# Splitting the key weights behind the first three query units, in the first group of an attention's projections

## The chip, the cores and the metric

The kernel runs on one core of a Trainium2 chip. The engines of that core are TensorE (PE in the profile, with its weight loads as PEld), VectorE (DVE), ScalarE (ACT), GpSimd (POOL) and SyncE (SP), which issues the DMAs. The metric is the device time of one execution in microseconds; less is better.

## The reference, cut to what matters

1024 tokens of width 512 pass through two "macaron" layers: half a feed-forward, an attention, half a feed-forward, each on a layer-normed input and added to the residual `x`. What the change touches is the start of the first layer's attention:

```python
q = hidden_states @ Wq + bq          # hidden 1024 x 512, Wq 512 x 4096
k = hidden_states @ Wk + bk
v = hidden_states @ Wv + bv
q = rms_norm(q, gq)                  # over all 4096 columns
k = rms_norm(k, gk)
...                                  # 32 heads of 128, softmax, values
return out @ Wo + bo
```

All of it is float32. The kernel multiplies at float32 accuracy by splitting both operands into a high part (rounded to a shorter format, `fp32r`) and a low part (the rest), and adding three matmuls: high by high, high by low, low by high.

## The kernel before

The program is a row of blocks with a barrier of all engines between them. The block in question is `qkv_block`. The 4096 columns of each projection are cut in 8 groups of 512 (4 heads). A group runs Q, then K, then V, each as 8 units; a unit is one 128x512 result in one PSUM bank (4 banks in turn), made by 12 matmuls of 512 columns (4 blocks of the width by 3 terms). Group 0 and group 7 are written out, groups 1 to 6 are a loop.

Each engine runs its own list in the order of the code, and waits on semaphores:

- TensorE, unit u: waits until the low part of this projection's weights is there (`w_lo_done`), and until three units less have been taken out of PSUM (`res_done` of at least u - 3 within group 0's Q), then 12 matmuls. In Q of group 0 the weights and the units 0 and 2 were already made at the end of the block before, so TensorE begins with unit 1, goes on with unit 3, and waits for nothing but `res_done` after that.
- VectorE, unit u: `qkv_res` (L826), the unit out of PSUM with the bias added, into one of 4 buffers; in Q then `qkv_q_lo` (L801) of unit u - 1, which needs ScalarE's `qkv_q_hi`.
- ScalarE, unit u: `qkv_q_hi` (L752), the high part of the query times the gain, then `qkv_sq` (L755), the square. The squares have two buffers, so the square of unit u waits until GpSimd has added the square of unit u - 2 (`acc_done`).
- GpSimd: clears its sums, waits for the output bias `bo` by DMA, adds it to the residual `x` in 8 instructions of 128x512 (L855), and only then starts on the group's squares, `qkv_acc` (L865), one per unit of Q and K.
- SyncE: the bias and gain columns, then the key weights `Wk`, `bo`, the value weights `Wv` and a bias; later the stores of the results to DRAM.

In front of each projection's units, ScalarE and VectorE split the weights of the *next* projection: ScalarE `qkv_w_hi` (L734, 128x2048), VectorE `qkv_w_lo` (L767, 128x2048). In group 0 the split in front of the query units is that of the key weights, which are at that time still on their way from DRAM.

Of the kernel before, what the change touches and what calls it, by code (L numbers as in the profile page):

```python
# [54 lines left out]
def wait(eng, sem, value):  # L55

    if isinstance(value, int) and value <= 0:
        return
    eng.wait_ge(sem, value)
# [560 lines left out]
def qkv_block(core, ins, scratch, first):  # L620
# [3 lines left out]
    with ExitStack() as ctx:  # L624
# [6 lines left out]
        Q, K, V = range(3)  # L631
# [26 lines left out]
        k_in, q_in, bo_in, bv_in = sem("k_in"), sem("q_in"), sem("bo_in"), sem("bv_in")  # L658
        kn_done, k0_hi_done = sem("kn_done"), sem("k0_hi_done")

        AT_SUMS, AT_SPREAD = 1, 3
        block = core.open_block(ctx)
        weights = [ins["Wq"], ins["Wk"], ins["Wv"]]
        bias, gain = [core.cols["bq"], core.cols["bk"]], core.cols["gq"]
# [1 line left out]
        def groups(eng, body):  # L666

            body(0)
            with eng.Fori(1, NGROUPS - 1) as g:
                body(g)  # L670
            body(NGROUPS - 1)

        def is_last(g):
            return isinstance(g, int) and g == NGROUPS - 1
# [54 lines left out]
        @block.scalar  # L729
        def _(act):  # L730
            def split(n, t, g):
                act.wait_ge(w_in[t], (g if t == Q else g + 1) * 16)
                wait(act, proj_done, (n - 2) * UNITS - 1)
                nc.scalar.activation(w_hi[t][:], w[t][:], ACT.Copy).then_inc(w_hi_done, 1)  # L734

            def body(g):
                for t in (Q, K, V):
                    n = g * 3 + t
                    if t < V:
                        split(n + 1, t + 1, g)  # L740
                    elif not is_last(g):
                        split(n + 1, Q, g + 1)
                    for u in range(UNITS):
                        if t == V:
                            continue
                        m = g * 16 + t * UNITS + u
                        act.wait_ge(res_done, n * UNITS + u + 1)
                        if t == Q:
                            if u == 0:
                                act.wait_ge(gain_done, g + 2)  # L750
                            wait(act, q_stored[u % 4], (g * 2 + u // 4) * 32)
                            nc.scalar.activation(q_hi[u % 4][:], res[u % 4][:], ACT.Copy,  # L752
                                                 scale=gain_now[:, u // 2:u // 2 + 1]).then_inc(q_hi_done, 1)
                        wait(act, acc_done, m + 2 - 1)
                        nc.scalar.activation(sq[:, u % 2, :], res[u % 4][:], ACT.Square).then_inc(sq_done, 1)  # L755

            groups(act, body)
            act.wait_ge(ms_done, 1)
            nc.scalar.activation(sd, ms, ACT.Sqrt).then_inc(sd_done, 1)
            act.wait_ge(kn_done, 1)  # L760
            nc.scalar.activation(core.first.hi[:], core.kn[:], ACT.Copy).then_inc(k0_hi_done, 1)

        @block.vector
        def _(v):
            def split(n, t):
                v.wait_ge(w_hi_done, n)
                nc.vector.tensor_tensor(w_lo[t][:], w[t][:], w_hi[t][:], ALU.subtract).then_inc(w_lo_done, 1)  # L767

            def factors():

                v.wait_ge(sums_done, 1)
                nc.vector.tensor_scalar(ms, core.bank(6)[:, 0:2 * NT].rearrange("p (a t) -> p a t", a=2),
                                        1.0 / INNER, RMS_EPS, ALU.mult, ALU.add).then_inc(ms_done, 1)
                v.wait_ge(sd_done, 1)
                nc.vector.reciprocal(r0, sd).then_inc(rs_done, 1)
                v.wait_ge(rs_done, 1)
                nc.vector.tensor_tensor(corr, ms, r0, ALU.mult).then_inc(rs_done, 1)
                v.wait_ge(rs_done, 2)
                nc.vector.tensor_tensor(corr, corr, r0, ALU.mult).then_inc(rs_done, 1)
                v.wait_ge(rs_done, 3)  # L780
                nc.vector.tensor_scalar(corr, corr, -0.5, 1.5, ALU.mult, ALU.add).then_inc(rs_done, 1)
                v.wait_ge(rs_done, 4)
                nc.vector.tensor_tensor(rs, r0, corr, ALU.mult).then_inc(rs_done, 1)
                v.wait_ge(rs_done, 5)

                nc.vector.tensor_scalar(core.rq, rs[:, 0, :], float(HD) ** -0.5, None,
                                        ALU.mult).then_inc(rms_done, 1)
                nc.vector.tensor_tensor(diag[:], core.ident[:].unsqueeze(1).broadcast_to([P, NT, P]),
                                        rs[:, 1, :].unsqueeze(2).broadcast_to([P, NT, P]), ALU.mult)\
                    .then_inc(diag_done, 1)  # L790

            v.wait_ge(core.cols_in, 16 * len(core.cols))
            nc.vector.tensor_tensor(gain, gain, core.cols["gk"], ALU.mult).then_inc(gain_done, 1)
            v.wait_ge(gain_done, 1)

            def next_gain(g):
                nc.vector.tensor_copy(gain_now, gain[:, bass.ds(g * GROUP, GROUP)]).then_inc(gain_done, 1)

            def q_low(g, u):
                v.wait_ge(q_hi_done, g * UNITS + u + 1)  # L800
                nc.vector.scalar_tensor_tensor(out=q_lo[u % 4][:], in0=res[u % 4][:],  # L801
                                               scalar=gain[:, bass.ds(g * GROUP + u // 2, 1)], in1=q_hi[u % 4][:],
                                               op0=ALU.mult, op1=ALU.subtract).then_inc(q_lo_done, 1)

            next_gain(0)

            def body(g):
                for t in (Q, K, V):
                    n = g * 3 + t
                    if t < V or not is_last(g):  # L810
                        split(n + 1, (t + 1) % 3)
                    for u in range(UNITS):
                        wait(v, proj_done, n * UNITS + u)
                        if 4 <= t * UNITS + u < UNITS + 4:
                            v.wait_ge(q_lo_done, g * UNITS + t * UNITS + u - 3)
                        else:
                            wait(v, stored[u % 4], (g * 4 + max(t * 2 - 2 + u // 4, 0)) * 16)
                        wait(v, sq_done, g * 16 + max(min(t * UNITS + u - 3, 16), 0))
                        if t == V:
                            if u == 0:  # L820
                                v.wait_ge(bv_in, (g + 1) * 16)
                                if not is_last(g):
                                    next_gain(g + 1)
                            nc.vector.tensor_tensor(res[u % 4][:], core.bank(u % 4), bv[:], ALU.add).then_inc(res_done, 1)  # L824
                        else:
                            nc.vector.tensor_scalar(res[u % 4][:], core.bank(u % 4),  # L826
                                                    bias[t][:, bass.ds(g * GROUP + u // 2, 1)], None, ALU.add)\
                                .then_inc(res_done, 1)
                            if t == Q and u >= 1:
                                q_low(g, u - 1)  # L830
                            elif t == K and u == 0:
                                q_low(g, UNITS - 1)
                        if is_last(g) and t == V and u == AT_SUMS + 1:
                            factors()
                        if is_last(g) and t == V and u == AT_SPREAD + 1:
                            v.wait_ge(spread_done, 1)
                            nc.vector.tensor_copy(core.rk[:], core.ps[2][:]).then_inc(rms_done, 1)

                            v.wait_ge(k_in, 16)
                            v.wait_ge(rms_done, 2)  # L840
                            nc.vector.tensor_tensor(core.kn[:], core.k_raw[:], core.rk[:], ALU.mult)\
                                .then_inc(kn_done, 1)

            groups(v, body)

        @block.gpsimd
# [983 lines left out]
```

## Time and profile before

| | us |
|---|---|
| median of 3 runs | 2322.78 |
| lowest, highest | 2320.69, 2324.09 |
| the profiled execution | 2324.25 |
| its span in the profile | 2322.5 |
| PE busy | 2256.0 (97%) |
| DVE, ACT, POOL busy | 1609.4, 1135.6, 828.8 |
| granted TensorE clock, mean | 0.989 |

The block of the projections takes the span from about 101 to 630 us, the part that the change touches from 101 to 140 us. All times below are microseconds from the start of the span. "Busy" of a matmul overlaps its neighbour's, so the rate of TensorE is read from the distance of the starts. The granted clock is 1.00 at 2.4 GHz and 0.50 at 1.2 GHz.

### The profile page before, as it was taken

To read this page: it belongs to the slowest core of one execution; us is meant where nothing else is said; L and a number is where in the kernel's file an instruction comes from. 1 tells how busy PE (TensorE), PEld (TensorE's weight loads), DVE (VectorE), ACT (ScalarE), POOL (GpSimd) and SP (SyncE) were. 2 spreads that over 40 slices of the span, in tenths; PEclk is the share of its full clock that TensorE was granted. 3 is DMA by queue.
4 is the path that set the end of the run, shared out by engine and by line. 5 is a ranking of instruction groups with operands and counts; after the bars stand their busy time and mean duration, and the time that the engine had idled before them with its cause. 6 is when DMAs were issued, how large, how long until landed. Compare 5 with 4: busy or idle time off the path is not lost. (4 is left out here: it accounts for less than half of the span.)

```text
span 2322.5 us, 34366 instructions
## 1 busy us (share of the span) xinstructions
PE 2256.0 (97%) x11044; PEld 1874.1 (81%) x11044; DVE 1609.4 (69%) x2654; ACT 1135.6 (49%) x1845; POOL 828.8 (36%) x736
## 2 busy tenths in 40 slices
PE   7899999999989999999999999999998999899998
PEld 5688888888778888888888888888886788687887
DVE  5544444444378888888888888888886665785765
ACT  3233332322266666666666666666663344352442
POOL 4553332233222222212212222222214466672565
PEclk9999999999999999999999999999999999999999
DMA  3155555455332211211221221221201111141210
GB/s 114 47 181 191 190 177 183 168 187 184 132 107 71 81 55 67 81 66 56 81 72 50 81 72 50 81 78 44 81 24 41 51 68 44 33 129 37 73 59 37
DMA packets 106182, 210.47 MB, mean 91 GB/s; under 512 B 9728, under 2 KB 42496, under 8 KB 102784
## 3 DMA queue, kind: packets, MB, share of 16 engines
q1 hardware_dynamic: 106112, 209.57, 26.9%
q8 instruction: 39, 0.64, 0.1%
q14 instruction: 31, 0.25, 0.0%
HBM read 140.33 MB, written 69.21 MB: 90 GB/s over the span
## 5 line engine op out<-in xcount | busy, mean ns | idle before, releaser
L1106 ACT ACTIVATE at_pT_hi<-ps 128x512 fp32r<-128x512 f32 x512 | 278.3, 595 | 352.3 <-PE ps L1210 352.2
L1148 DVE TENSOR_REDUCE at_small<-ps 128x1 f32<-128x1024 f32 x256 | 312.5, 1221 | 84.0 <-PE ps L402 83.0
L1158 DVE TENSOR_TENSOR at_pT_lo<-ps,at_pT_hi 128x512 fp32r<-128x512 f32 x512 | 327.1, 680 | 3.8 <-ACT at_pT_hi L1106 3.8
L1113 ACT ACTIVATE at_probs<-ps,at_small,cols 128x1024 f32<-128x1024 f32 x256 | 309.2, 1208 | 28.2 <-DVE at_small L1150 21.6
L865 POOL TENSOR_TENSOR qkv_acc<-qkv_acc,qkv_sq 128x512 f32<-128x512 f32 x128 | 166.2, 1299 | 320.1 <-ACT qkv_sq L755 316.5
L1210 PEld LDWEIGHTS ps<-ident,at_probs 128*128 128x128 f32 x2048 | 239.2, 140 | 37.9 <-issue 4.4
L1210 PE MATMUL ps<-ident,at_probs 128*128 128x128 f32 x2048 | 266.4, 273 | 3.2 <-DVE at_pT_lo L1158 3.2
L1172 DVE SCALAR_TENSOR_TENSOR x<-ps,at_small,x 128x512 f32<-128x512 f32 x256 | 192.0, 750 | 10.2 <-PE ps L402 3.1
L1043 POOL TENSOR_TENSOR at_o_lo<-at_o_raw,at_o_hi 128x512 fp32r<-128x512 f32 x32 | 41.2, 1288 | 439.8 <-ACT at_o_hi L1127 439.8
L402 PE MATMUL ps<-ln_xT_hi,ln_xT_lo 128*128 128x512 f32 x768 | 196.0, 390 | 0.0
L826 DVE TENSOR_SCALAR qkv_res<-ps,cols 128x512 f32<-128x512 f32 x128 | 94.9, 748 | 141.7 <-PE ps L402 122.7
L1235 PE MATMUL ps<-at_pT_hi,ln_xT_lo 128*128 128x512 f32 x512 | 180.6, 393 | 0.7 <-DVE at_y_lo L1144 0.7
L402 PEld LDWEIGHTS ps<-ln_xT_hi,ln_xT_lo 128*128 128x128 f32 x768 | 144.2, 188 | 30.7
L402 PE MATMUL ps<-ln_xT_hi,q_hi 128*128 128x512 f32 x480 | 148.0, 390 | 0.0
L752 ACT ACTIVATE qkv_q_hi<-qkv_res,cols 128x512 fp32r<-128x512 f32 x64 | 46.3, 723 | 194.6 <-DVE qkv_res L826 194.6
L755 ACT ACTIVATE qkv_sq<-qkv_res 128x512 f32<-128x512 f32 x128 | 80.0, 625 | 121.3 <-DVE qkv_res L826 104.8
L402 PE MATMUL ps<-at_o_hi,at_y_hi 128*128 128x512 f32 x256 | 122.0, 477 | 3.9 <-DVE x L1172 3.5
L402 PE MATMUL ps<-ln_xT_hi,first_hi 128*128 128x512 f32 x280 | 113.3, 405 | 7.1 <-DVE ln_xT_lo L282 4.0
L1043 POOL TENSOR_TENSOR ln_xT_hi<-kn,ln_xT_hi 128x1024 fp32r<-128x1024 f32 x31 | 74.2, 2393 | 116.0 <-ACT ln_xT_hi L1083 116.0
L1235 PEld LDWEIGHTS ps<-at_pT_hi,ln_xT_lo 128*128 128x128 f32 x512 | 96.0, 188 | 22.1 <-issue 0.9
L824 DVE TENSOR_TENSOR qkv_res<-ps,qkv_bv 128x512 f32<-128x512 f32 x64 | 43.5, 688 | 98.9 <-PE ps L402 98.8
L402 PE MATMUL ps<-ln_xT_hi,first_lo 128*128 128x512 f32 x280 | 111.1, 397 | 0.0
(273 smaller groups left out, 5636.4 us busy)
## 6 DMA issues: line engine op xcount, KB each, us to landing
scratch_q_hi<-qkv_q_hi SPq DMA_DIRECT2D x64, 256.0 KB, 2.1
scratch_q_lo<-qkv_q_lo SPq DMA_DIRECT2D x64, 256.0 KB, 2.3
scratch_k<-qkv_res SPq DMA_DIRECT2D x64, 256.0 KB, 2.8
scratch_v<-qkv_res SPq DMA_DIRECT2D x64, 256.0 KB, 2.3
k_raw<-scratch_k SPq DMA_DIRECT2D x32, 512.0 KB, 3.8
at_v_raw<-scratch_v SPq DMA_DIRECT2D x32, 512.0 KB, 3.3
wq_raw<-in_Wq SPq DMA_DIRECT2D x8, 1024.0 KB, 6.5
qkv_w<-in_Wk SPq DMA_DIRECT2D x8, 1024.0 KB, 5.0
```

The costliest lines, as they stand in the source:

```text
L402: last = nc.tensor.matmul(out, s, m, start=(start and n == 0), stop=(stop and n == len(terms) - 1))
L755: nc.scalar.activation(sq[:, u % 2, :], res[u % 4][:], ACT.Square).then_inc(sq_done, 1)
L826: nc.vector.tensor_scalar(res[u % 4][:], core.bank(u % 4), bias[t][:, bass.ds(g * GROUP + u // 2, 1)], None, ALU.add)\
L865: nc.gpsimd.tensor_tensor(part, part, sq[:, u % 2, :], ALU.add).then_inc(acc_done, 1)
L1043: nc.gpsimd.tensor_tensor(dst, a, b, ALU.subtract).then_inc(done, 1)
L1106: nc.scalar.activation(pT2[jp][0][:, 4 * b:4 * b + 4, w * P:(w + 1) * P], T_BANKS[:, b * HALF:(b + 1) * HALF].rearrange("p (k n) -> p k n" ...
L1113: nc.scalar.activation(probs[l % 4][:], scores(l)[:], ACT.Exp, bias=nbias[:, l % 4:l % 4 + 1], scale=rq[:, l % NT:l % NT + 1], accum_out=s ...
L1148: nc.vector.reduce_max(maxes[:, l % 4:l % 4 + 1], scores(l)[:], AX.X).then_inc(s_max, 1)
L1158: nc.vector.tensor_tensor(pT2[jp][1][out], T_BANKS[:, b * HALF:(b + 1) * HALF].rearrange("p (k n) -> p k n", k=4), pT2[jp][0][out], ALU.su ...
L1172: nc.vector.scalar_tensor_tensor(out=x[:, tile, :], in0=core.bank(WO_BANK), scalar=rsums[:, c:c + 1], in1=x[:, tile, :], op0=ALU.mult, op1 ...
L1210: last = nc.tensor.transpose(T_BANKS[:, k * P:(k + 1) * P], probs[(l - T_LAG) % 4][:, k * P:(k + 1) * P], core.ident[:])
L1235: last = nc.tensor.matmul(core.bank(PV_BANK), a[:, k, :], b[:, k, :], start=(c == 0 and n == 0), stop=(c == 3 and n == len(terms) - 1))
```

## The change

In Q of group 0 alone (`late`), ScalarE and VectorE no longer split the key weights ahead of unit 0, but between unit 2 and unit 3 (`LATE` is 3). The instructions are the same, 1845 on ScalarE and 2654 on VectorE; nothing of another group moves, and the code of TensorE, GpSimd and SyncE is as it was.

```diff
-        AT_SUMS, AT_SPREAD = 1, 3
+        AT_SUMS, AT_SPREAD, LATE = 1, 3, 3
...
 # ScalarE
                 for t in (Q, K, V):
                     n = g * 3 + t
-                    if t < V:
+                    late = isinstance(g, int) and g == 0 and t == Q
+                    if t < V and not late:
                         split(n + 1, t + 1, g)
-                    elif not is_last(g):
+                    elif t == V and not is_last(g):
                         split(n + 1, Q, g + 1)
                     for u in range(UNITS):
+                        if late and u == LATE:
+                            split(n + 1, t + 1, g)
...
 # VectorE
-                    if t < V or not is_last(g):
+                    late = isinstance(g, int) and g == 0 and t == Q
+                    if not late and (t < V or not is_last(g)):
                         split(n + 1, (t + 1) % 3)
                     for u in range(UNITS):
+                        if late and u == LATE:
+                            split(n + 1, t + 1)
```

ScalarE's list at the start of the block, with the semaphores that each instruction waits on (`qkv_w1` are the key weights, the number in `qkv_res2` is the unit's buffer). Before:

```order
L734 ACTIVATE qkv_w1_hi<-qkv_w1 128x2048 [waits qkv_w_in1]
L752 ACTIVATE qkv_q_hi0<-qkv_res0,cols 128x512 [waits qkv_gain_done,qkv_res_done]
L755 ACTIVATE qkv_sq<-qkv_res0 128x512 [waits qkv_acc_done]
L752 ACTIVATE qkv_q_hi1<-qkv_res1,cols 128x512 [waits qkv_res_done]
L755 ACTIVATE qkv_sq<-qkv_res1 128x512 [waits qkv_acc_done]
L752 ACTIVATE qkv_q_hi2<-qkv_res2,cols 128x512 [waits qkv_res_done]
L755 ACTIVATE qkv_sq<-qkv_res2 128x512 [waits qkv_acc_done]
L752 ACTIVATE qkv_q_hi3<-qkv_res3,cols 128x512 [waits qkv_res_done]
```

The same place after:

```order
L755 ACTIVATE qkv_q_hi0<-qkv_res0,cols 128x512 [waits qkv_gain_done,qkv_res_done]
L758 ACTIVATE qkv_sq<-qkv_res0 128x512 [waits qkv_acc_done]
L755 ACTIVATE qkv_q_hi1<-qkv_res1,cols 128x512 [waits qkv_res_done]
L758 ACTIVATE qkv_sq<-qkv_res1 128x512 [waits qkv_acc_done]
L755 ACTIVATE qkv_q_hi2<-qkv_res2,cols 128x512 [waits qkv_res_done]
L758 ACTIVATE qkv_sq<-qkv_res2 128x512 [waits qkv_acc_done]
L734 ACTIVATE qkv_w1_hi<-qkv_w1 128x2048 [waits qkv_w_in1]
L755 ACTIVATE qkv_q_hi3<-qkv_res3,cols 128x512 [waits qkv_res_done]
```

The high part of the key weights now stands behind the squares of the units 0, 1 and 2. (Lines from L736 on carry a number higher by 3 or more in the kernel after.)

VectorE's list at the same place. Before:

```order
L767 TENSOR_TENSOR qkv_w1_lo<-qkv_w1,qkv_w1_hi 128x2048 [waits qkv_w_hi_done]
L826 TENSOR_SCALAR qkv_res0<-ps0,cols 128x512
L826 TENSOR_SCALAR qkv_res1<-ps0,cols 128x512 [waits qkv_proj_done]
L801 SCALAR_TENSOR_TENSOR qkv_q_lo0<-qkv_res0,cols,qkv_q_hi0 128x512 [waits qkv_q_hi_done]
L826 TENSOR_SCALAR qkv_res2<-ps1,cols 128x512 [waits qkv_proj_done]
L801 SCALAR_TENSOR_TENSOR qkv_q_lo1<-qkv_res1,cols,qkv_q_hi1 128x512 [waits qkv_q_hi_done]
L826 TENSOR_SCALAR qkv_res3<-ps1,cols 128x512 [waits qkv_proj_done]
```

After:

```order
L832 TENSOR_SCALAR qkv_res0<-ps0,cols 128x512
L832 TENSOR_SCALAR qkv_res1<-ps0,cols 128x512 [waits qkv_proj_done]
L804 SCALAR_TENSOR_TENSOR qkv_q_lo0<-qkv_res0,cols,qkv_q_hi0 128x512 [waits qkv_q_hi_done]
L832 TENSOR_SCALAR qkv_res2<-ps1,cols 128x512 [waits qkv_proj_done]
L804 SCALAR_TENSOR_TENSOR qkv_q_lo1<-qkv_res1,cols,qkv_q_hi1 128x512 [waits qkv_q_hi_done]
L770 TENSOR_TENSOR qkv_w1_lo<-qkv_w1,qkv_w1_hi 128x2048 [waits qkv_w_hi_done]
L832 TENSOR_SCALAR qkv_res3<-ps1,cols 128x512 [waits qkv_proj_done]
```

The low part of the key weights moved from ahead of the first `qkv_res` to just ahead of the fourth, and its wait for the high part moved with it.

## Rows read from the trace of the kernel before

**Rows 1.** Busy time of each engine over the span, from the page.

```profile
PE 2256.0 (97%) x11044; PEld 1874.1 (81%) x11044; DVE 1609.4 (69%) x2654; ACT 1135.6 (49%) x1845; POOL 828.8 (36%) x736
```

**Rows 2.** Waits of PE, whole span: who, for whom, us in total, times, longest.

```profile
PE ps L402 <- DVE qkv_res L826: 6.9, 1, 6.9
```

**Rows 3.** PE in order of time: start, duration, instruction, [idle before, its releaser].

```profile
106.91 0.39 PE L402 MATMUL ps<-ln_xT_hi,wq_lo 128*128 128x512 f32 x1
114.24 0.80 PE L402 MATMUL ps<-ln_xT_hi,wq_hi 128*128 128x512 f32 x1 [6.94 <-DVE qkv_res L826]
114.83 0.63 PE L402 MATMUL ps<-ln_xT_lo,wq_hi 128*128 128x512 f32 x1
...
119.52 0.46 PE L402 MATMUL ps<-ln_xT_hi,wq_hi 128*128 128x512 f32 x1
...
125.08 0.39 PE L402 MATMUL ps<-ln_xT_hi,wq_hi 128*128 128x512 f32 x1
...
127.80 0.39 PE L402 MATMUL ps<-ln_xT_hi,qkv_w_hi 128*128 128x512 f32 x1
...
138.80 0.50 PE L402 MATMUL ps<-ln_xT_hi,qkv_w_hi 128*128 128x512 f32 x1
```

**Rows 4.** ScalarE and VectorE at the start of the block, same columns.

```profile
104.96 0.17 DVE L797 COPY cols<-cols 128x4 f32<-128x4 f32 x1
108.58 1.91 ACT L734 ACTIVATE qkv_w_hi<-qkv_w 128x2048 fp32r<-128x2048 f32 x1 [8.03 <-DMA qkv_w<-in_Wk]
110.52 3.00 DVE L767 TENSOR_TENSOR qkv_w_lo<-qkv_w,qkv_w_hi 128x2048 fp32r<-128x2048 f32 x1 [5.39 <-ACT qkv_w_hi L734]
113.44 1.40 DVE L826 TENSOR_SCALAR qkv_res<-ps,cols 128x512 f32<-128x512 f32 x2
124.76 0.63 ACT L755 ACTIVATE qkv_sq<-qkv_res 128x512 f32<-128x512 f32 x1 [6.90 <-POOL qkv_acc L865]
```

**Rows 5.** GpSimd in windows of 1 to 2 us; first add, second, last.

```profile
110.11 1.26 POOL L855 TENSOR_TENSOR x<-x,qkv_bo 128x512 f32<-128x512 f32 x1 [6.33 <-DMA qkv_bo<-in_bo]
111.33 3.32 POOL L855 TENSOR_TENSOR x<-x,qkv_bo 128x512 f32<-128x512 f32 x1
...
119.24 1.74 POOL L855 TENSOR_TENSOR x<-x,qkv_bo 128x512 f32<-128x512 f32 x1
120.94 1.29 POOL L855 TENSOR_TENSOR x<-x,qkv_bo 128x512 f32<-128x512 f32 x1
...
123.44 1.28 POOL L865 TENSOR_TENSOR qkv_acc<-qkv_acc,qkv_sq 128x512 f32<-128x512 f32 x1
```

**Rows 6.** ScalarE and VectorE around the split of the value weights.

```profile
133.08 0.63 ACT L755 ACTIVATE qkv_sq<-qkv_res 128x512 f32<-128x512 f32 x1 [0.45 <-POOL qkv_acc L865]
133.62 1.90 ACT L734 ACTIVATE qkv_w_hi<-qkv_w 128x2048 fp32r<-128x2048 f32 x1
135.55 2.53 DVE L767 TENSOR_TENSOR qkv_w_lo<-qkv_w,qkv_w_hi 128x2048 fp32r<-128x2048 f32 x1 [3.65 <-ACT qkv_w_hi L734]
138.00 0.74 DVE L826 TENSOR_SCALAR qkv_res<-ps,cols 128x512 f32<-128x512 f32 x1
```

**Rows 7.** All splits of VectorE by line: min/median/max ns, first and last start.

```profile
L767 DVE TENSOR_TENSOR qkv_w_lo<-qkv_w,qkv_w_hi x16: 2281/2292/2996, 110.5 to 589.1; 128x2048 fp32r<-128x2048 f32 x16
```

**Rows 8.** Stretches: length, busy of PE, PEld, DVE, ACT, POOL, clock, DMA, GB/s.

```profile
652.00:653.00 1.00, 0.86 (x4) 0.89 (x5) 0.62 (x2) 0.94 (x2) 1.00 (x1) 0.56 0.00 0
653.00:654.00 1.00, 1.00 (x7) 1.00 (x6) 1.00 (x2) 0.60 (x1) 1.00 (x1) 0.50 0.91 242
...
655.00:656.00 1.00, 1.00 (x4) 0.72 (x4) 0.77 (x3) 0.90 (x2) 0.00 (x0) 0.74 0.00 0
...
614.00:615.00 1.00, 1.00 (x9) 1.00 (x9) 0.00 (x0) 0.00 (x0) 0.00 (x0) 0.78 1.03 352
615.00:617.00 2.00, 2.00 (x10) 2.00 (x11) 0.00 (x0) 0.00 (x0) 0.00 (x0) 0.50 0.57 172
...
621.00:622.00 1.00, 1.00 (x5) 0.78 (x5) 0.06 (x1) 0.00 (x0) 0.00 (x0) 0.80 0.00 0
```

## The prediction

> **What bounds the kernel now.** I read the totals first: PE is busy 97% of the span [rows 1], so a change can only pay where PE stands still or runs at its lower clock. Next the list of who waited for whom: it has one wait of PE for `qkv_res` in the whole program [rows 2], and the order of time shows where [rows 3]: PE makes query units 1 and 3, the last matmul of these starts at 106.91, and then it idles 6.94 us, released by `qkv_res` at 114.24. The matmuls behind that start 0.43 us apart instead of 0.23 (114.83 is the second of twelve), the lower clock, until 119.52, where unit 5 begins.
>
> The chain behind the wait is in [rows 4]. VectorE had its columns at 104.96 and could have taken unit 0 out of PSUM then. But first in its list stands the low part of the key weights; that waits for the high part on ScalarE (108.58), and that for the DMA of `Wk`. So the first `qkv_res` starts at 113.44, and PE 0.80 later. From there on PE runs without a gap to the key units (127.80), and past them, but for a short wait at the fifth key unit: it starts at 138.80, where four units of 2.72 behind 127.80 give 138.68, and its first matmul takes 0.50 instead of 0.39, so 0.2 in all.
>
> The other fact that counts lies off this chain. GpSimd starts adding `bo` to `x` at 110.11, when that DMA has landed, and reaches the first square at 123.44 [rows 5]. ScalarE's third square has to wait for it: it starts at 124.76 after 6.90 us of idling [rows 4]. Today PE doesn't feel this. In the changed kernel the split stands behind exactly this square.
>
> **The change, part by part.** Nothing is added or removed, and the time is decided by one event, the start of the first key unit on PE: 127.80 now.
>
> 1. *The old wait goes.* The first `qkv_res` starts at about 105.1, right behind 104.96, and takes 0.7. Unit 4 needs it when PE is done with unit 3, at 106.91 + 0.23 = 107.14. There is 1.3 us to spare, so the 6.94 us of idling go, and so does the slow stretch behind it (12 matmuls in 119.52 - 114.24 = 5.28, against 127.80 - 125.08 = 2.72 at the full clock: 2.56 us). Unit 5 needs the second result and unit 6 the third; VectorE and ScalarE have these by 109, since only `qkv_q_hi`, the square and `qkv_q_lo` of two units lie between. PE makes the units 4, 5 and 6 from 107.14 to 107.14 + 3 x 2.72 = 115.30.
>
> 2. *A new wait comes.* Unit 7 needs the fourth result, `qkv_res` of unit 3, and VectorE has now the low part of the key weights in front of it, which waits for the high part on ScalarE, which stands behind the third square, which waits for the first `qkv_acc` on GpSimd, which stands behind eight adds of `bo`. `Wk` itself has landed by 108.58 and is no longer what is waited for. Step by step:
>  - GpSimd starts at 110.11, as now. Its adds last 13.33 now (110.11 to 123.44), but the undisturbed ones are 1.25 apart (from 120.94 to 123.44 two of them). The second took 3.32 beside VectorE's 3.00 us split, the middle ones 1.7 beside VectorE's `qkv_q_lo` [rows 4, 5]. After the change VectorE has nothing to do from about 109 until the split, so I take 8 x 1.25 = 10.0: 120.1.
>  - The first `qkv_acc` and the hand-over to ScalarE: 124.76 - 123.44 = 1.32 [rows 4, 5]. Third square at 121.4.
>  - Square to high part: 133.62 - 133.08 = 0.54. High part to low part: 135.55 - 133.62 = 1.93. Low part to the next `qkv_res`: 138.00 - 135.55 = 2.45 with a duration of 2.53; the usual one is 2.29 [rows 6, 7], and GpSimd is out of squares to add by about then, so 2.2. `qkv_res` to PE: 0.80 [rows 3, 4]. Sum 5.5: PE goes on at 126.9.
>  - The stall is 126.9 - 115.3 = 11.6 us, in place of 6.94.
>
> 3. *The lower clock comes back.* After an idle time longer than today's, PE will again start at 0.50. The cost is that of the same 12 matmuls, 2.56 us. From both sides: elsewhere the clock was at 0.50 from about 652.1 to 655.5, a loss of 1.7, and from about 614.8 to 621.2 [rows 8] (0.22 + 0.20 + 6 x 0.50), a loss of 3.4.
>
> 4. *Sum.* Unit 7 takes 2.72 + 2.56 = 5.28, the first key unit starts at 126.9 + 5.3 = 132.2, against 127.80: +4.4. The short wait of 0.2 at the fifth key unit goes, as VectorE gets to the first key unit little later than now: today the third and the eighth square start at 124.76 and 133.08 [rows 4, 6], so 1.66 apart; in the changed kernel the fourth starts at about 127.9, the eighth at 134.5, and the first key result at 139.5 instead of 138.00, while PE asks for it at 132.2 + 4 x 2.72 = 143.1. Net **+4.2 us**. From there on PE waits for no result until the projections end [rows 2], so the loss is carried to the end. On the profiled execution's own time that is 2324.25 + 4.2 = 2328.5; that execution lay 1.5 above the median of the runs shown, so for the median I say 2322.78 + 4.2 = **2327.0 us**, 0.18% more.
>
> The moved work also shifts the stores. SyncE sends the first two units' queries (four stores of 256 KB) some 9 us earlier, while `bo` and `Wv` are on their way. If these stores took bandwidth from `bo`, GpSimd would start later: with the DMAs full they move 352 GB/s [rows 8], so 256 KB take 0.75 us, and two such stores are issued before `bo` lands: 0 to 1.5 us. They stand behind `bo` in the same queue, so I take 0. The other stores, and the load of the next `Wq` behind them in SyncE's queue, wait for the third query's low part, now past 126; the last of them depends on VectorE's first key unit, which is 1.5 later at most, and PE, which would use `Wq` 24 units on, is 4.2 later itself.
>
> A rule of the Trainium skill bears on the 10.0 us. GpSimd's eight adds stretched when VectorE ran operations with two inputs in SBUF (3.32 beside 3.00) and not otherwise (1.25) [rows 4, 5]. The page "SBUF — State Buffer", section "Who interferes with whom", says that such a VectorE instruction and a GpSimd instruction that reads SBUF block one another for the whole instruction; the trace agrees, and by this rule the sum is +4.2. Without it, the adds would last 13.3 and the sum would be +7.5.
>
> **The rivals.**
>
> *A: the adds don't get faster.* If what slowed them was the DMA traffic of that time and not VectorE, GpSimd reaches the squares at 123.4 as now, and everything in step 2 is 3.3 later: +7.5, 2330.3 us, slower by 0.32%. For it: the second add also ran while `Wv` landed. Against it: the adds of 1.74 fell together with `qkv_q_lo`, and those from 120.94 on with none, both beside stores. 1 in 10.
>
> *B: the stall goes, and no new one comes.* Then the gain is 6.94 + 2.56 = 9.5 us: 2313.3, faster by 0.4%. It needs the first `qkv_acc` to end by 115.3 - 5.5 = 109.8, so that the fourth result is there in time. But the adds can't even start before `bo` has landed, at 110.11. It could only come if the third square didn't wait for it, and 6.90 us of idling [rows 4] say that it does. 1 in 25.
>
> *C: both stalls weigh the same.* If the clock came back early after the new wait (a loss of 1.7) and the adds ran 1.22 apart, as the first two did (110.11, 111.33), the sum is about +3; nothing measurable. If it came back late (3.4) or `bo` was late by 1.5, it is +5 to +6.5. This is the width of my own forecast.
>
> **How the numbers follow.** Forecast, stall with free adds: 8 in 10, its own range +2.5 to +6, 2325.3 to 2328.8. A: 1 in 10, 2330.3. B: 0.04. The rest for what I don't see. A measurement of this kernel can tell 0.2%, 4.65 us, from no change. My sum of 4.2 lies just inside that bound; of the forecast's 0.8 I give 0.3 to a sum above it. With A that makes slower 0.40; faster 0.05 (B and a little); within the bound 0.55. The range goes from 2324.0 (the low end of the forecast, less the spread of the medians, since three runs of before lay 3.4 apart) to 2330.5 (rival A).
>
> **What would show it.** In the profile after: no idle time of PE at 107; matmuls 0.23 apart to 115.3; then an idle time of 11 to 12 us, released by `qkv_res`; ScalarE's third square at about 121.4, released by `qkv_acc`, the split right behind; the eight adds in 10.0 us; the clock at 0.50 at the restart; the first key unit at about 132. I am wrong if PE stands still before 115, if the third square doesn't wait, or if a second stall shows up between 132 and 145.

## The result, and the profile after

| | before | after |
|---|---|---|
| median of 10 runs, us | 2323.2 | 2328.44 |
| lowest, highest | 2320.69, 2325.47 | 2325.08, 2330.42 |
| the profiled execution | 2324.25 | 2328.15 |
| its span | 2322.5 | 2326.4 |

The medians lie 5.2 us apart. The ratio is 1.0021 with a 95% interval of 1.0011 to 1.0031, so the changed kernel takes 4.9 us more, between 2.6 and 7.2; a second set of runs of the same kernel further down (e5) gave 1.0024 (1.0015 to 1.0033), 4.7 us by the medians. Both intervals leave out no change, and both hold the forecast's 4.2 us: the kernel is slower, by an amount that can't be told from the forecast.

The totals say nothing of it: PE is busy 97% as in [rows 1].

TensorE after the change, in order of time (start, duration, instruction, [idle before, its releaser]); the rows that answer to [rows 3]:

```profile
102.05 0.47 PE L402 MATMUL ps<-ln_xT_hi,wq_hi 128*128 128x512 f32 x1 [0.30 <-PEq L461]
...
115.53 0.39 PE L402 MATMUL ps<-ln_xT_hi,wq_lo 128*128 128x512 f32 x1
127.47 0.79 PE L402 MATMUL ps<-ln_xT_hi,wq_hi 128*128 128x512 f32 x1 [11.56 <-DVE qkv_res L832]
128.07 0.63 PE L402 MATMUL ps<-ln_xT_lo,wq_hi 128*128 128x512 f32 x1
...
130.61 0.40 PE L402 MATMUL ps<-ln_xT_lo,wq_hi 128*128 128x512 f32 x1
...
131.77 0.39 PE L402 MATMUL ps<-ln_xT_hi,qkv_w_hi 128*128 128x512 f32 x1
...
142.65 0.39 PE L402 MATMUL ps<-ln_xT_hi,qkv_w_hi 128*128 128x512 f32 x1
```

The wait of 6.94 us ahead of unit 4 is gone: units 4, 5 and 6 follow without a gap up to 115.53. In its place stands one of 11.56 us ahead of unit 7, released by the same instruction of VectorE. The block began 0.45 later than in before (102.05; the same matmul of before started at 101.60), so times of the two traces are to be compared less 0.45. The first key unit starts at 131.77, the fifth at 142.65, 3.85 behind the 138.80 of before, and the span is 3.9 longer. So what is lost here is carried to the end: 3.4 from start to fifth key unit, and 0.45 by the later start.

ScalarE, VectorE and GpSimd after, same columns; they answer to [rows 4 to 6]:

```profile
105.46 1.40 DVE L832 TENSOR_SCALAR qkv_res<-ps,cols 128x512 f32<-128x512 f32 x2
...
108.33 0.74 DVE L804 SCALAR_TENSOR_TENSOR qkv_q_lo<-qkv_res,cols,qkv_q_hi 128x512 fp32r<-128x512 f32 x1
124.29 2.47 DVE L770 TENSOR_TENSOR qkv_w_lo<-qkv_w,qkv_w_hi 128x2048 fp32r<-128x2048 f32 x1 [15.21 <-ACT qkv_w_hi L734]
126.68 0.74 DVE L832 TENSOR_SCALAR qkv_res<-ps,cols 128x512 f32<-128x512 f32 x1
...
121.83 0.63 ACT L758 ACTIVATE qkv_sq<-qkv_res 128x512 f32<-128x512 f32 x1 [12.59 <-POOL qkv_acc L871]
122.36 1.89 ACT L734 ACTIVATE qkv_w_hi<-qkv_w 128x2048 fp32r<-128x2048 f32 x1
...
110.67 9.90 POOL L861 TENSOR_TENSOR x<-x,qkv_bo 128x512 f32<-128x512 f32 x8 [6.44 <-DMA qkv_bo<-in_bo]
120.53 4.08 POOL L871 TENSOR_TENSOR qkv_acc<-qkv_acc,qkv_sq 128x512 f32<-128x512 f32 x3
```

To be read from the bottom: GpSimd's eight adds end at 120.53, its first sum lets ScalarE's third square go at 121.83, the high part of the key weights follows at 122.36, the low part at 124.29 after VectorE has idled for 15.21 us, and the fourth `qkv_res` at 126.68. Before, ScalarE idled 6.90 us for the same sum, and TensorE felt nothing of it but the short wait at the fifth key unit.

### The profile page after: what moved, and what is told of

Read it like the earlier page. It is cut to its first block and busy times, and to the rows that moved or that the text cites. A ratio compares the mean times of both kernels' runs of the same rounds, so it can differ in the third digit from the quotient of the medians.

```text
span 2326.4 us, 34366 instructions
## 1 busy us (share of the span) xinstructions
PE 2254.3 (97%) x11044; PEld 1873.0 (81%) x11044; DVE 1602.6 (69%) x2654; ACT 1135.6 (49%) x1845; POOL 825.0 (35%) x736
## 5 line engine op out<-in xcount | busy, mean ns | idle before, releaser
L402 PE MATMUL ps<-ln_xT_hi,first_hi 128*128 128x512 f32 x280 | 113.6, 406 | 7.0 <-DVE ln_xT_lo L282 4.0
L402 PE MATMUL ps<-ln_xT_hi,wq_hi 128*128 128x512 f32 x256 | 100.8, 394 | 11.9 <-DVE qkv_res L832 11.6
```

Of the source, the lines that this page charges most:

```text
L402: last = nc.tensor.matmul(out, s, m, start=(start and n == 0), stop=(stop and n == len(terms) - 1))
```

## The experiments

Every time below is the median of 5 to 11 runs, beside runs of before on the same chip. Executions of one kernel lie up to 8 us apart (before, beside e1 to e4: 2319.89 to 2327.63), so each row has a second measure, from the trace: the distance from TensorE's first matmul in the block to its first matmul of the fifth key unit, the last place in the block where any of these kernels waits for `qkv_res`. Before it is 138.80 - 101.60 = 37.20.

One thing that moves the time of an execution shows in all twelve traces. Near the end of the block, where TensorE has waited for nothing since the fifth key unit, the granted clock falls to 0.50 once more [rows 8]. That costs 3.4 us in some executions and 1.7 in others, of one and the same program too. After and e5, the same columns as in [rows 8]:

```profile
616.00:627.00 11.00, 11.00 (x52) 9.59 (x51) 1.79 (x5) 0.21 (x1) 0.00 (x0) 0.69 0.34 117
```

```profile
616.00:627.00 11.00, 11.00 (x59) 9.53 (x58) 2.27 (x8) 0.22 (x1) 0.00 (x0) 0.84 0.45 153
```

It is 3.4 in before, after, e1, e2, e3, e4 and e6, and 1.7 in e5, e7, e8, e9 and e10. Why it differs is open.

| | ratio to before (95%) | median, before beside it | to the fifth key unit |
|---|---|---|---|
| after | 1.0021 (1.0011-1.0031) | 2328.44, 2323.2 | 40.60 |
| e1, adds behind | 0.9955 (0.9941-0.9968) | 2313.81, 2323.78 | 27.30 |
| e2, before, adds behind | 1.0004 (0.9995-1.0013) | 2324.19, 2323.78 | 36.60 |
| e3, LATE = 2 | 0.9996 (0.9987-1.0005) | 2323.57, 2323.78 | 36.87 |
| e4, split ahead of the third square | 1.0002 (0.9993-1.0011) | 2323.93, 2323.78 | 36.38 |
| e5, after again | 1.0024 (1.0015-1.0033) | 2328.65, 2323.99 | 41.53 |
| e6, `bo` first | 1.0014 (1.0005-1.0023) | 2327.35, 2323.99 | 39.60 |
| e7, `bo` behind | 1.0034 (1.0021-1.0048) | 2332.53, 2323.99 | 45.40 |
| e8, busy stall | 1.0010 (1.0001-1.0019) | 2326.65, 2323.99 | 39.32 |
| e9, four squares | 1.0000 (0.9991-1.0008) | 2323.76, 2323.51 | 33.91 |
| e10, e1 again | 0.9957 (0.9943-0.9971) | 2314.57, 2323.51 | 27.28 |

### Take the adds away from in front: e1 and e2

```diff
 # GpSimd
-            pool.wait_ge(bo_in, 16)
-            for t in range(NT):
-                nc.gpsimd.tensor_tensor(core.x[:, t, :], core.x[:, t, :], bo[:], ALU.add)
             def body(g):
                 ...
+                if isinstance(g, int) and g == 0:
+                    pool.wait_ge(bo_in, 16)
+                    for t in range(NT):
+                        nc.gpsimd.tensor_tensor(core.x[:, t, :], core.x[:, t, :], bo[:], ALU.add)
```

> The changed kernel, with GpSimd's eight adds of bo to x moved from ahead of group 0's squares to behind them (GpSimd has nothing to do in the value units). My theory (the split waits for the third square, and that for the adds): the third square starts at about 109.3, the split of the key weights at 109.8, VectorE's low part at 111.7, the fourth qkv_res at 113.9, so TensorE goes on at 115.3 without a stall, its clock stays at 1.00, and the first key unit starts at about 118 instead of 127.8: 10 us below before, 2313. Rival (any split behind unit 2 comes too late for TensorE, whoever holds it up): a stall of several us remains and the time is within 3 us of before.

> The kernel before with the same move of the adds on GpSimd and nothing else. My theory: TensorE's 6.94 us wait hangs on the DMA of Wk, not on GpSimd, so it stays; only VectorE's low part of the key weights loses its neighbour (3.00 to 2.29 us), so 0.7 to 1 us below before, not to be told from it. Rival (the adds alone cost the time, wherever the split stands): it gains most of the 10 us as well.

e1, the list of TensorE's waits between 101 and 160 us (who, for whom, us in total, times, longest), then the same instructions as above:

```profile
PE ps L402 <- PEq L461: 0.3, 1, 0.3
```

```profile
108.59 0.62 ACT L758 ACTIVATE qkv_sq<-qkv_res 128x512 f32<-128x512 f32 x1
109.11 1.90 ACT L734 ACTIVATE qkv_w_hi<-qkv_w 128x2048 fp32r<-128x2048 f32 x1
...
111.04 2.62 DVE L770 TENSOR_TENSOR qkv_w_lo<-qkv_w,qkv_w_hi 128x2048 fp32r<-128x2048 f32 x1 [2.12 <-ACT qkv_w_hi L734]
113.58 0.74 DVE L832 TENSOR_SCALAR qkv_res<-ps,cols 128x512 f32<-128x512 f32 x1
...
142.96 12.09 POOL L870 TENSOR_TENSOR x<-x,qkv_bo 128x512 f32<-128x512 f32 x8
```

With the adds out of the way the third square follows the second at once, the split is done by 113.6, and TensorE has no wait but that at the block's start. The kernel is 10 us faster than before (2313.81 against 2323.78), where 10 were expected. In e10, the same kernel once more, it is 8.9, where 8.5 to 11.5 were expected. The eight adds are still made, from 142.96 on, when GpSimd has no squares to add.

The same edit in the kernel before does nothing that can be measured. TensorE's wait there is 6.2 us instead of 6.94:

```profile
PE ps L402 <- DVE qkv_res L826: 6.2, 1, 6.2
...
110.17 2.29 DVE L767 TENSOR_TENSOR qkv_w_lo<-qkv_w,qkv_w_hi 128x2048 fp32r<-128x2048 f32 x1 [5.46 <-ACT qkv_w_hi L734]
```

That is the 0.7 us by which the low part gets faster when GpSimd isn't adding (2.29 in place of 3.00). The rival, by which the adds alone cost the time, is out. So neither edit alone gains: the split's move alone costs 5 us, the adds' move alone gives 0, and both together give 10.

### Move the split by one place: e3 and e4

```diff
-        AT_SUMS, AT_SPREAD, LATE = 1, 3, 3
+        AT_SUMS, AT_SPREAD, LATE = 1, 3, 2
```

> The changed kernel with LATE = 2: both engines split the key weights ahead of unit 2 instead of unit 3, so the split no longer stands behind the third square, which is the first one that needs GpSimd. My theory: the high part at 108.6 as in before, the low part at 110.5 beside GpSimd's adds, the third qkv_res at 113.4, TensorE stalls 1.6 us ahead of unit 6; then the third square, at about 123.5 behind the adds, holds up the fourth high part, its qkv_q_lo and the sixth result, so a second stall of about 4 us ahead of the second key unit. Sum 2 us below before (between 0 and 4), 7 below the changed kernel. Rival (the loss comes from splitting late as such): between before and the changed kernel, 2324 to 2328.

And e4, on ScalarE alone:

```diff
-                        if late and u == LATE:
-                            split(n + 1, t + 1, g)
                         ...
+                        if late and u == LATE - 1:
+                            split(n + 1, t + 1, g)
                         wait(act, acc_done, m + 2 - 1)
```

> The changed kernel with one swap on ScalarE: the high part of the key weights stands ahead of the third square (behind its qkv_q_hi) instead of behind it; VectorE as in the changed kernel, ahead of unit 3. My theory: the high part at 109.2, the low part at 111.1 to 114, the fourth qkv_res at about 114, TensorE does unit 7 at 115.3 without a stall; the third square is still at 122 to 123 and holds up the sixth result to about 125.5, so TensorE stalls some 5 us ahead of the second key unit, at 120.8, and restarts at the lower clock. Sum 3 us below before (1 to 5), 8 below the changed kernel. Rival (it is VectorE's place of the low part that costs, not ScalarE's queue): as the changed kernel, 2328.

Both are rid of the 5 us that the change costs, and neither gains over before: 0.2 below and 0.2 above, where I had expected 2 and 3 below. e4's rival, as slow as the changed kernel, fails. e3's rival, that a late split loses as such and the time lies between before and after (2324 to 2328), can't be told apart by e3's own time of 2323.6; what speaks against it is e1, where the split stands as late as in the changed kernel and 10 us are gained. The traces show the stalls where I had put them, and a further one. First e3, then e4, TensorE:

```profile
114.69 0.50 PE L402 MATMUL ps<-ln_xT_hi,wq_hi 128*128 128x512 f32 x1 [1.67 <-DVE qkv_res L832]
...
127.47 0.80 PE L402 MATMUL ps<-ln_xT_hi,qkv_w_hi 128*128 128x512 f32 x1 [4.32 <-DVE qkv_res L832]
...
138.72 0.50 PE L402 MATMUL ps<-ln_xT_hi,qkv_w_hi 128*128 128x512 f32 x1 [0.16 <-DVE qkv_res L832]
```

```profile
126.19 0.79 PE L402 MATMUL ps<-ln_xT_hi,qkv_w_hi 128*128 128x512 f32 x1 [5.84 <-DVE qkv_res L832]
...
137.43 0.50 PE L402 MATMUL ps<-ln_xT_hi,qkv_w_hi 128*128 128x512 f32 x1 [1.39 <-DVE qkv_res L832]
```

The last row of each is the start of the fifth key unit. ScalarE's third square, released by GpSimd's first sum:

```profile
124.73 0.63 ACT L758 ACTIVATE qkv_sq<-qkv_res 128x512 f32<-128x512 f32 x1 [9.34 <-POOL qkv_acc L871]
```

```profile
123.45 0.63 ACT L758 ACTIVATE qkv_sq<-qkv_res 128x512 f32<-128x512 f32 x1 [13.42 <-POOL qkv_acc L871]
```

The distance from this square to the fifth key unit is 138.72 - 124.73 = 13.99 in e3, 137.43 - 123.45 = 13.98 in e4, and 138.80 - 124.76 = 14.04 in before. It is a chain of fixed length: five more squares at GpSimd's pace of 1.7 us, then the split of the value weights and the first key result. The kernel before has **two bounds that end within 0.2 us of each other**: the DMA of `Wk` through the split in front, and the adds of `bo` through the squares. I had read the short wait at 138.80 (0.12 us behind the 138.68 of an undisturbed run of units) as a leftover, when it was the second bound already deciding. Whatever takes the first away while the second stands gains nothing.

### How strongly `bo` decides: e5, e6, e7

> The changed kernel itself once more, beside the three that follow. Both theories: 5 us above before (4 to 6), TensorE's stall 11.6 us.

e6 issues the DMA of `bo` ahead of `Wk`, e7 behind `Wv` and the value bias:

```diff
 # e6                                       # SyncE
+            sp.dma_start(bo[:], ins["bo"].partition_broadcast(P)).then_inc(bo_in, 16)
             load(0, K)
-            sp.dma_start(bo[:], ins["bo"].partition_broadcast(P)).then_inc(bo_in, 16)
```

> The changed kernel, with the DMA of bo issued ahead of that of Wk instead of behind it: bo should land near 107 instead of 110.7, Wk 0.7 us later. My theory: GpSimd's adds start 3.5 to 4 us earlier, lose 0.5 to 1 of that beside VectorE's two qkv_q_lo, and TensorE's stall shrinks by 3 us, to about 8.5; time 3 us below the changed kernel, 1 to 2 above before. Rival (the split waits for Wk): no gain, since Wk lands later.

> The changed kernel, with the DMA of bo issued behind Wv and the bias of the values: bo should land near 114 instead of 110.7. My theory: everything behind the adds is 3 us later, stall 14.5 to 15 us, time 3 us above the changed kernel (2331 to 2332), 8 above before. Rival (the split waits for Wk, which lands 0.7 us earlier or as before): as the changed kernel.

GpSimd's adds in e5, e6 and e7, with the wait for `bo` ahead of them:

```profile
110.68 9.90 POOL L861 TENSOR_TENSOR x<-x,qkv_bo 128x512 f32<-128x512 f32 x8 [6.43 <-DMA qkv_bo<-in_bo]
```

```profile
112.63 9.93 POOL L861 TENSOR_TENSOR x<-x,qkv_bo 128x512 f32<-128x512 f32 x8 [5.20 <-DMA qkv_bo<-in_bo]
```

```profile
116.19 9.82 POOL L862 TENSOR_TENSOR x<-x,qkv_bo 128x512 f32<-128x512 f32 x8 [10.11 <-DMA qkv_bo<-in_bo]
```

The wait counts from the end of GpSimd's clearing, so it hardly hangs on when the block began. It is 6.43, 5.20 and 10.11: `bo` came 1.23 earlier in e6 and 3.68 later in e7. TensorE's stall follows one for one:

```profile
PE ps L402 <- DVE qkv_res L832: 11.6, 1, 11.6
```

```profile
PE ps L402 <- DVE qkv_res L832: 10.3, 1, 10.3
```

```profile
PE ps L402 <- DVE qkv_res L833: 15.2, 1, 15.2
```

and the distance to the fifth key unit goes the same way, 1.9 shorter than in e5 in e6 and 3.9 longer in e7. The medians are 1.3 less than e5's in e6, which lies within the noise (the two intervals overlap), and 3.9 more in e7. Both rivals wanted the stall to hang on `Wk`. The size that I expected of e6, 3 us, failed on one point: `bo` first in the queue doesn't land 3.5 to 4 us earlier, but 1.2. The mechanism held. `Wk` landed later in e6 (7.5 us after issue instead of 5.4), some 9 us ahead of the split at 124.35, so its DMA is no bound here.

### The lower clock: e8

```diff
                         if start and u == UNITS - 1:      # TensorE, ahead of unit 7's wait
+                            for i in range(44):
+                                nc.tensor.matmul(core.bank(7), w_hi[t][:, i % KB, 0:HD], xT.hi[:, i % KB, 0:HALF],
+                                                 start=True, stop=True)
```

> The changed kernel, with 44 matmuls of 512 columns more on TensorE ahead of query unit 7, into a PSUM bank that nobody reads: 10 us of work in the 11.6 us in which it idles. My theory of the lower clock as a price of the idle time: the restart is as early as before, but at the full clock, so the time is 1.5 to 3.4 us below the changed kernel, 2 to 3 above before. Rival (the lower clock costs nothing, it is hidden behind VectorE's pace): as the changed kernel.

TensorE in and at the end of the stall, in e8:

```profile
115.86 10.13 PE L906 MATMUL ps<-ln_xT_hi,wq_hi 128*128 128x512 f32 x44
127.74 0.50 PE L402 MATMUL ps<-ln_xT_hi,wq_hi 128*128 128x512 f32 x1 [1.75 <-DVE qkv_res L832]
...
130.60 0.39 PE L402 MATMUL ps<-ln_xT_hi,qkv_w_hi 128*128 128x512 f32 x1
```

The granted clock from 100 to 140 us is 1.00 in e8 and 0.87 in after:

```profile
100.00:140.00 40.00, 37.95 (x169) 30.87 (x168) 18.15 (x22) 14.07 (x19) 23.60 (x19) 1.00 0.44 159
```

```profile
100.00:140.00 40.00, 28.14 (x119) 22.59 (x118) 17.62 (x22) 14.05 (x19) 23.38 (x19) 0.87 0.44 159
```

Unit 7 takes 2.86 us instead of 4.30 in the profile after and 5.20 in that of e5 (127.49 to 132.69), though it starts no earlier. So the lower clock is a price of its own, on top of the idle time: that rests on these traces. The median is 2.0 below e5's, within the expected 1.5 to 3.4, but the intervals of the two overlap (1.0001 to 1.0019, 1.0015 to 1.0033), so by the times alone it isn't shown.

### The squares' buffers: e9

```diff
         sq = sb("sq", [P, 2, HALF])
+        squares = [sq[:, 0, :], sq[:, 1, :], core.kn[:, 0:HALF], core.kn[:, HALF:TOK]]
...
-                        wait(act, acc_done, m + 2 - 1)
-                        nc.scalar.activation(sq[:, u % 2, :], ...
+                        wait(act, acc_done, m + 2 - 3)
+                        nc.scalar.activation(squares[u % 4], ...
```

GpSimd's sum reads from `squares[u % 4]` likewise.

> The changed kernel with four buffers for the squares instead of two (the two new ones lie in kn, which is free until the last group), so that the square of unit u waits for GpSimd's sum of unit u - 4 and not u - 2; GpSimd's adds stay ahead of the squares. My theory: the third and the fourth square no longer wait, the split of the key weights is made at 110 to 114 us and TensorE's 11.6 us stall ahead of unit 7 is gone. But from e3 and e4 I now hold that GpSimd sets a second bound: there the fifth key unit started 14.0 us behind the third square, as in before, whatever stood ahead. Here the first square that waits is the fifth, at about 124.8, and the fifth key unit should start 10.5 us behind it (14.0 less two squares of 1.7), at 135 instead of 138.8, with stalls of 1.5 us ahead of the fourth and 5 us ahead of the fifth key unit and the lower clock behind them. Time 1 us below before (3 below to 1 above), 6 below the changed kernel. Rival (the stall has to do with the split's place alone, not with the squares' buffers): as the changed kernel.

ScalarE's fifth square and TensorE's two waits:

```profile
124.69 0.63 ACT L759 ACTIVATE qkv_sq<-qkv_res 128x512 f32<-128x512 f32 x1 [8.15 <-POOL qkv_acc L872]
```

```profile
127.44 0.50 PE L402 MATMUL ps<-ln_xT_hi,qkv_w_hi 128*128 128x512 f32 x1 [1.36 <-DVE qkv_res L833]
...
135.26 0.50 PE L402 MATMUL ps<-ln_xT_hi,qkv_w_hi 128*128 128x512 f32 x1 [4.77 <-DVE qkv_res L833]
135.92 0.63 PE L402 MATMUL ps<-ln_xT_hi,qkv_w_lo 128*128 128x512 f32 x1
...
139.72 0.40 PE L402 MATMUL ps<-ln_xT_hi,qkv_w_hi 128*128 128x512 f32 x1
```

The stall of 11.6 us is gone with nothing moved, only by taking the third square's reason to wait away; that settles the link between the square and the split. And the second bound shows as forecast: the fifth key unit starts 135.26 - 124.69 = 10.57 behind the first square that waits, with 10.5 expected. Counted from the block's start it begins 3.3 earlier than in before, but after 4.77 us of idling, and what follows runs at the lower clock: the sixth key unit starts 4.46 behind the fifth instead of 2.72 (139.72 is its first matmul), which takes 1.7 of the 3.3 back. The time is that of before, within 2 us.

## Why the prediction was right

*The old wait goes.* Right. The first `qkv_res` started at 105.46 (105.0 less the block's shift, 105.1 said), and TensorE's last matmul before the new stall at 115.53, so its end of work at 115.3 on the clock of before, as said.

*The new wait.* Right in every link. Beside the terms of the sum:

| term | said | measured |
|---|---|---|
| eight adds | 10.0 | 120.53 - 110.67 = 9.86 |
| first sum to third square | 1.32 | 121.83 - 120.53 = 1.30 |
| square to high part | 0.54 | 0.53 |
| high part to low part | 1.93 | 1.93 |
| low part to `qkv_res` | 2.2 | 126.68 - 124.29 = 2.39 |
| `qkv_res` to TensorE | 0.80 | 127.47 - 126.68 = 0.79 |
| stall | 11.6 | 127.47 - 115.76 = 11.71; 11.56 of it idle |

(115.76 is where the next matmul would have started, 0.23 behind 115.53, as the forecast's 115.3 is.) The low part took 2.47 and not 2.29: GpSimd's third sum was still running, since its three sums took 4.08 from 120.53 on. That the sum of the terms came out within about 0.1 is in part luck: the adds were 0.14 shorter than said, the low part 0.19 longer.

*The adds get faster, rival A.* Right to take 10.0, and A is refuted. Two stretches of the kernel after (length; busy time of PE, PEld, DVE, ACT, POOL with the number of instructions; granted clock, DMA share, GB/s):

```profile
112.00:114.00 2.00, 2.00 (x11) 1.65 (x10) 0.00 (x0) 0.00 (x0) 2.00 (x2) 1.00 1.00 391
...
116.00:118.00 2.00, 0.00 (x0) 0.00 (x0) 0.00 (x0) 0.00 (x0) 2.00 (x2) 1.00 0.00 0
```

The adds ran at the same pace with the DMAs full (391 GB/s) and with none. With VectorE's split beside them they don't: in e3 the longest of the eight took 3.324 us, in e4 3.338, in after 1.290. First e3, then after (shortest, median, longest in ns):

```profile
L861 POOL TENSOR_TENSOR x<-x,qkv_bo x8: 1272/1284/3324, 110.5 to 122.2; 128x512 f32<-128x512 f32 x8
...
L861 POOL TENSOR_TENSOR x<-x,qkv_bo x8: 1259/1275/1290, 110.7 to 119.3; 128x512 f32<-128x512 f32 x8
```

The rule of the Trainium skill ("SBUF — State Buffer", section "Who interferes with whom") that a VectorE instruction with two inputs in SBUF and a GpSimd instruction that reads SBUF block one another agrees with these rows: 3.32 us beside the split, 1.29 at most with VectorE idle.

*The lower clock.* Right in kind; the size varies between executions of one program. The clock stood at 0.50 at the restart and came back during unit 7, in after:

```profile
128.00:129.00 1.00, 1.00 (x4) 0.74 (x3) 1.00 (x3) 0.92 (x3) 0.23 (x1) 0.50 0.04 16
...
130.00:131.00 1.00, 1.00 (x4) 0.77 (x4) 1.00 (x2) 0.92 (x3) 0.86 (x2) 0.71 1.08 389
```
 The loss on unit 7 was 4.30 - 2.72 = 1.6 us in the profile after and 5.20 - 2.72 = 2.5 in that of e5, inside the bounds of 1.7 and 3.4 but for a tenth; 2.56 was said.

*The stores.* Right in effect: GpSimd's wait for `bo` is 6.44 against 6.33, so 0.1 of the 0 to 1.5. The count was wrong: all four stores, and not two, were issued before `bo` landed at 110.6 (107.78, 108.17, 109.10, 109.47), so the small effect rests on more than was said. Not seen was that the eighth `qkv_q_hi` would wait 1.1 us for the store of the fourth query; TensorE asked for what depends on it 2.5 us after it was there.

*The sum.* +4.2 was said for the start of the fifth key unit. Measured at that place it is +3.4 in after and +4.3 in e5, 3.9 on the mean; the medians say 5.2 and 4.7. The traces belong to single executions. That of before lay 1.05 above its median and that of after 0.29 below, which accounts for the distance from 3.9 (the difference of the two spans) to 5.2. That of e5 lay 1.6 below its median, and it is one of those that lost only 1.7 us to the clock near the block's end. The forecast median was 2327.0, the measured one 2328.44. The prediction gave 0.40 to a loss above 4.65 us and 0.55 to a difference within that bound; the medians lie so close to that line that these runs don't decide between the two.

*Rival B.* It had its condition right: the gain needs the first sum to be out of the way. e1 met that condition. To the fifth key unit it gained 37.20 - 27.30 = 9.90; B's 9.5 left out the short wait and counted the old one by its idle time of 6.94, where from start to start it costs 114.24 - 107.14 = 7.10. What the prediction lacked was the step to e3 and e4: that before stands on two bounds of the same height.

## What to carry to other kernels

Before an instruction is moved down an engine's list, look at what each instruction that it now stands behind waits for, also when those waits cost nothing today: an idle time off the critical path (ScalarE's 6.90 us here) becomes the bound for all that is queued behind it. And when a change that removes a plain stall brings nothing, look for a second chain that ends at about the same time; a wait of 0.1 to 0.2 us further down was its sign here. Work that nobody needs soon (here `bo` onto `x`, used only in the next block) belongs behind the work that others wait for; that move, together with the change, made the fastest of these kernels.

## What the runs showed of the hardware

The load of `bo` to all partitions (256 KB, read 128 times from 2 KB) took 6.3 us from issue to landing behind the megabyte of `Wk`, 5.5 ahead of it (e6) and 9.0 behind `Wv` and a bias (e7). The stores of the first queries, of 256 KB too and issued 3.5 to 5.2 us behind it, took 6.6 and 6.8 in after, though the stores of that kind take 2.1 and 2.3 in the median of the whole program. How much of the 5.5 us is the load's own and how much the traffic of that stretch, no run here separates. A stall of the same 11.6 us in the same program cost 1.6 us of lower clock in one execution and 2.5 in another, and the stretch at 0.50 near the block's end 3.4 and 1.7; so single traces of one program can lie 1 to 2 us apart by the clock alone.
